# A selective-scan kernel: pairs of state groups scanned in one VectorE instruction over two PSUM banks

## The chip, the cores and the metric

The kernel runs on one core of a Trainium2 chip. The metric is the device time of one execution in microseconds; times are medians of several runs on the same chip. A profile is one execution, recorded by the hardware profiler.

## The reference, cut to what matters

One transformer-like layer on x of 2 x 2048 tokens with 256 features: a modulated layer norm, a bidirectional Mamba mixer, and a mixture of experts. The change touches the mixer's recurrence alone. For each direction it is

```python
def step(h, inp):                       # h: (batch, 512, 16)
    dt_t, u_t, B_t, C_t = inp
    h = h * jnp.exp(dt_t[:, :, None] * A) + (dt_t * u_t)[:, :, None] * B_t[:, None, :]
    y = jnp.einsum('bdn,bn->bd', h, C_t)
    return (h, y)
_, ys = jax.lax.scan(step, h0, xs)      # 2048 tokens, h0 = 0
```

So every one of 512 x 16 states is a first-order recurrence over the tokens: decay times the previous value, plus an input. The result is weighted with C and summed over the 16 states.

## The kernel before, in words

**Steps and units.** The tokens are cut into 8 blocks of 512 (four per batch entry), and forward and backward passes alternate, so there are 16 steps q: even ones forward, odd ones backward. In each step the 512 x 16 states are laid on 128 partitions as 16 units; a unit is four groups (i = 0 to 3) of 128 states, each with 512 tokens along the row. Four units make a chunk of 128 inner channels. All work of the scan stage is counted by the unit T (q = T // 16, t = T % 16). Steps 0, 1, 8 and 9 begin a sequence, so their states start at zero (`q // 2 % SEG == 0`); the other twelve start from states that an earlier step has stored.

**One unit passes through four engines.**
- ScalarE (`decay`, L1225) writes exp(A dt) of group i into PSUM bank PS_A + i, 128x512, four times a unit. It may write a bank when the scan that read it four scans ago is done (`scan_done`).
- VectorE (`multiply`, L1516) writes dbu = (dt u) B, 128x2048, from a PSUM bank and `b_rep` in SBUF. For units t = 3, 7, 9, 11 and 15 (`POOL_UNITS`) GpSimd does it instead (L898), with both inputs in SBUF.
- VectorE (`scan`, L1530) runs the recurrence of one group over 512 tokens: first input the decays in PSUM, second input `dbu` in SBUF, start value 0.0 or a column of `state`, result in the ring `hst` of 7 units.
- ScalarE (`save_state`, L1213) copies the last column of `hst` to `state` (where a later step needs it: all but steps 6, 7, 14 and 15). GpSimd (`weigh`, L910) then multiplies the unit of `hst` in place with `c_rep`; it waits for the scans and for that copy. TensorE (`sum_chunk`, L1949) sums a chunk in PSUM, and VectorE's `gate_y` (L1509) multiplies that with the gate.

**Order.** Every engine's program is written out by hand. VectorE in slot T: the multiplication for unit T+1 (unless it is GpSimd's), then the four scans of T, with a `gate_y` at t = 2, 8, 11 and 15. GpSimd in slot T: the multiplication for T+2 if that is one of its five, then the weighing of T-1, then at four places of a step a 128x512 product (`step_input`, L890). `dbu` has three buffers, so GpSimd's multiplication for T+2 waits for the scans of T-1. ScalarE in slot T: four decays, with the copy of the state of T-1 before the last, and between them its other work (convolution outputs, softplus, SiLU) at (t, n) places given by small tables. TensorE's projections, convolutions and sums run beside.

**Around the stage.** Ahead of it stand the norms (VectorE L1475 to L1496, with GpSimd helping), behind it the experts. The last unit's weighing is VectorE's (L1700).

## Time and profile before

| what | us |
|---|---|
| median of 3 runs | 2182.23 |
| lowest, highest | 2181.46, 2185.82 |
| the profiled execution | 2187.26 |
| its span in the trace | 2185.5 |
| VectorE busy | 2001.1 (92%) |
| GpSimd busy | 1813.4 (83%) |
| TensorE busy | 1896.7 (87%) |
| ScalarE busy | 1390.7 (64%) |

The scan stage reaches from 84 to 1705 us. The page divides the span into 40 slices, of which slices 2 to 31 are this stage. Busy time is the union of an engine's instructions; a duration includes a tail that the next instruction overlaps, so the distance between starts is a little less than the duration.

### The profile page before, as it was taken

What the parts mean: (1) busy time and instruction counts of PE and PEld (TensorE: products, weight loads), DVE (VectorE), ACT (ScalarE), POOL (GpSimd) and SP (SyncE); (2) the same over time, 40 slices, a digit from 0 to 9 for tenths busy, and PEclk for the clock granted to TensorE, in tenths of its full rate; (3) what the DMA queues carried; (4) which work ended last, traced back from release to release, by engine and by line L of the source; (5) the groups of instructions that cost most, each with busy time, mean ns of one, the idle gap of its engine ahead of it and who ended that gap; (6) DMA issues with size and microseconds to landing.
All of it is one profiled execution on the core that took longest, in us unless ns stands there. A gap on an engine that the chain in (4) does not pass through costs nothing.

```text
span 2185.5 us, 25009 instructions
## 1 busy us (share of the span) xinstructions
PE 1896.7 (87%) x6376; PEld 804.2 (37%) x6377; DVE 2001.1 (92%) x2325; ACT 1390.7 (64%) x2540; POOL 1813.4 (83%) x625
## 2 busy tenths in 40 slices
PE   7879898988889898989888898988775799999997
PEld 3323232323233332324232333333221466655554
DVE  7889999999999999999999999999999777557776
ACT  5777868677767768686877777676755333434443
POOL 5599999999999999999999999999999343415444
PEclk9889898989889898989898998989876799999999
DMA  6754535353635444453536253454433552235444
GB/s 257 244 140 123 125 105 126 100 134 86 149 88 131 110 115 120 113 126 105 125 100 150 82 138 99 120 121 113 102 95 133 210 202 81 100 78 84 78 78 69
DMA packets 140339, 265.26 MB, mean 121 GB/s; under 512 B 21264, under 2 KB 44048, under 8 KB 139072
## 3 DMA queue, kind: packets, MB, share of 16 engines
q1 hardware_dynamic: 125488, 242.05, 40.7%
q0 software_dynamic: 13440, 17.93, 4.9%
q10 hardware_dynamic: 1296, 3.93, 0.5%
q8 instruction: 48, 0.79, 0.1%
q14 instruction: 67, 0.55, 0.1%
HBM read 194.51 MB, written 70.39 MB: 121 GB/s over the span
## 4 chain that ended last, share of the span: by engine, by line
DVE 39%; PE 23%; issue 13%; POOL 10%; DMA 6%; ACT 4%; DVEq 2%; SPq 2%; POOLq 0%; ACTq 0%; PEldq 0%
DVE hst L1530 28%; DVE dbu L1516 7%; POOL hst L910 5%; PE psum L2105 5%; POOL dbu L898 4%; PE psum L1949 3%; PE psum L2168 2%; DMA bc_scratch<-sp_tmp 2%; PE psum L2117 2%; PE psum L1869 2%; PE psum L1881 2%; DMA b_rep<-bc_scratch 1%; ACT psum L1225 1%; DVE sz L1509 1%; PE psum L1934 1%
## 5 line engine op out<-in xcount | busy, mean ns | idle before, releaser
L910 POOL TENSOR_TENSOR hst<-hst,c_rep 128x2048 f32<-128x2048 f32 x255 | 1149.8, 4539 | 12.0 <-ACT state L1213 11.4
L1225 ACT ACTIVATE psum<-dt_rep,neg_a 128x512 f32<-128x512 f32 x1024 | 691.4, 684 | 375.5 <-DVE hst L1530 374.2
L1530 DVE TENSOR_TENSOR_SCAN hst<-psum,state,dbu 128x512 f32<-128x512 f32 x768 | 918.3, 1258 | 0.0
L1516 DVE TENSOR_TENSOR dbu<-psum,b_rep 128x2048 f32<-128x2048 f32 x176 | 398.5, 2264 | 8.6 <-PE psum L1934 8.5
L898 POOL TENSOR_TENSOR dbu<-dtu_rep,b_rep 128x2048 f32<-128x2048 f32 x80 | 364.3, 4554 | 29.9 <-DVE hst L1530 29.9
L1934 PE MATMUL psum<-dt,same 32*128 32x512 f32 x352 | 216.4, 696 | 119.2 <-DVE dbu L1516 111.2
L1530 DVE TENSOR_TENSOR_SCAN hst<-psum,dbu 128x512 f32<-128x512 f32 x256 | 291.7, 1199 | 8.1 <-ACT psum L1225 8.1
L1949 PE MATMUL psum<-hst,same 128*32 128x512 f32 x2048 | 258.4, 649 | 16.6 <-POOL hst L910 8.8
L1881 PE MATMUL psum<-xp,taps 128*128 128x512 f32 x512 | 241.2, 615 | 12.4 <-ACT sp_tmp L1196 12.4
L1020 POOL DMA_INDIRECT out_x<-h,target_u x72 | 113.1, 1571 | 154.8 <-DMA out_x<-h,target_u 78.0
L1881 PEld LDWEIGHTS psum<-xp,taps 128*128 128x128 f32 x512 | 96.2, 195 | 153.5 <-issue 153.1
L2168 PE MATMUL psum<-w,h 128*128 x288 | 143.0, 619 | 7.9 <-DVE h L1775 2.2
L984 POOL DMA_INDIRECT slot_scratch<-send,slot_u x64 | 64.3, 1005 | 102.4 <-ACT send L1399 79.4
L1934 PEld LDWEIGHTS psum<-dt,same 32*128 32x128 f32 x352 | 56.1, 197 | 249.6 <-issue 152.2
L1949 PEld LDWEIGHTS psum<-hst,same 128*32 128x32 f32 x2048 | 63.5, 118 | 216.0 <-issue 186.0
L1915 PE MATMUL psum<-sp_tmp,w_dt 16*128 16x512 f32 x128 | 91.9, 832 | 55.8 <-ACT sp_tmp L1181 45.9
L1862 PE MATMUL psum<-xnT,w_in 128*128 128x512 f32 x256 | 126.7, 621 | 8.8 <-ACT xc L1167 7.7
L1869 PE MATMUL psum<-xnT,w_in 128*128 128x512 f32 x256 | 121.3, 606 | 0.6 <-ACT xc L1167 0.6
L1897 PE MATMUL psum<-w_out,sz 128*128 128x256 f32 x512 | 121.1, 391 | 0.0
L2105 PE MATMUL psum<-h2T,sw 128*128 128x512 f32 x256 | 115.0, 603 | 0.9 <-ACT g_silu L1385 0.9
L1897 PEld LDWEIGHTS psum<-w_out,sz 128*128 128x128 f32 x512 | 101.5, 198 | 30.1 <-issue 17.0
L1775 DVE TENSOR_TENSOR h<-psum,b 128x512 f32<-128x512 f32 x72 | 49.8, 691 | 51.0 <-issue 37.1
(183 smaller groups left out, 2418.3 us busy)
## 6 DMA issues: line engine op xcount, KB each, us to landing
dt_rep<-dt_scratch SPq DMA_DIRECT2D x256, 256.0 KB, 4.8
dtu_rep<-dtu_scratch SPq DMA_DIRECT2D x320, 64.0 KB, 1.9
taps<-taps_scratch SPq DMA_DIRECT2D x64, 256.0 KB, 3.2
b_rep<-bc_scratch SPq DMA_DIRECT2D x64, 256.0 KB, 5.0
c_rep<-bc_scratch SPq DMA_DIRECT2D x64, 256.0 KB, 7.8
dt_scratch<-dt SPq DMA_DIRECT2D x63, 256.0 KB, 4.7
h<-slot_scratch SPq DMA_DIRECT2D x72, 129.5 KB
sp_tmp<-t_scratch SPq DMA_DIRECT2D x16, 512.0 KB, 6.8
```

The lines of the kernel that those rows point to most:

```text
L898: nc.gpsimd.tensor_tensor(dbu[:, U % DBU, :, :], dtu_rep[:].broadcast_to((P, NG, TB)), b_rep[U // UNITS % 2][:], ALU.mult).then_inc(pool_m ...
L910: nc.gpsimd.tensor_tensor(h, h, c_rep[q % 2][:], ALU.mult).then_inc(prod_done, 1)
L1225: nc.scalar.activation(psum[:, PS_A + i, :], dt_rep[:, G % 2, j, :], ACT.Exp, scale=neg_a[:, q % 2, u, i:i + 1]).then_inc(exp_done, 1)
L1516: nc.vector.tensor_tensor(dbu[:, U % DBU, :, :], psum[:, PS_U:PS_U + 1, :].broadcast_to((P, NG, TB)), b_rep[U // UNITS % 2][:], ALU.mult). ...
L1530: nc.vector.tensor_tensor_scan(time_order(hst[:, U % RING, i, :], backward), time_order(psum[:, PS_A + i, :], backward), time_order(dbu[:, ...
L1869: ins = nc.tensor.matmul(psum[:, bank, :], w_in[:, q % 2, k, DI + c * P:DI + (c + 1) * P], xnT[:, q % 2, k, :], start=(k == 0), stop=(k == ...
L1881: ins = nc.tensor.matmul(psum[:, bank, :], taps[:, c % 2, j, :], xp[:, c % 2, at:at + TB], start=(j == 0), stop=(j == TAPS - 1))
L1897: ins = nc.tensor.matmul(psum[:, bank, half * DM:(half + 1) * DM], sz[:, c, tok], w_out[:, q % 2, c, :], start=False, stop=(half == 1 and ...
L1934: nc.tensor.matmul(psum[:, PS_U, :], same[part, :], dtu[part, c, :], start=True, stop=True).then_inc(u_full, 1)
L1949: ins = nc.tensor.matmul(psum[CH * j:CH * (j + 1), PS_Y, :], same[:, 0:CH], hst[:, (GN * G + j) % RING, i, :], start=False, stop=(i == NG ...
L2105: ins = nc.tensor.matmul(psum[:, bank, :], w[:, k, c * P:(c + 1) * P], h2T[:, j % 2, k, :], start=(k == 0), stop=(k == KD - 1))
L2168: ins = nc.tensor.matmul(psum[:, 2 + r % 2, :], xtT[:, r % 2, k * P:(k + 1) * P], w13[:, bass.ds(e * KD + k, 1), :].rearrange("p a n -> p ...
```

## The change

One scan instruction takes two groups: 1024 elements a row, over two neighbouring PSUM banks, two rows of `dbu` and two of `hst`. Its start value is always 0.0. So that the second group doesn't continue from the first one's end, the first decay of the second group (in the direction of time) is set to zero in PSUM: `no_decay` writes it once for each pair at t = 0 of a step, and the decays of those banks write 511 columns from then on. Stored states now enter through `dbu`: for each chunk of a step that starts from stored states, ScalarE computes exp(A dt) of the first token (`first_decays`, four 128x4 instructions), VectorE multiplies the 16 stored columns of the chunk by it (`scale_states`, 128x16, in place), and for each unit VectorE adds four columns to the first column of `dbu` (`add_seed`, 128x4). All tensors of these two are in SBUF. ScalarE now computes two decays in a row when a pair of banks is free, the copy of the state moves ahead of them, and two places of softplus move by one.

```diff
-DT_AT = [(10, 0), (10, 3), (12, 0), (13, 1)]
-COPY_DT_AT = [(11, 2), (12, 2), (13, 3), (15, 2)]
+FIRST_DT_AT = [(10, 0), (10, 3), (12, 0), (13, 1)]
+DT_AT = [(9, 3), (10, 3), (12, 1), (13, 1)]
+COPY_DT_AT = [(11, 1), (12, 2), (13, 3), (15, 2)]
...
-                nc.scalar.activation(psum[:, PS_A + i, :], dt_rep[:, G % 2, j, :], ACT.Exp,
+                kept = slice(0, TB) if i % 2 == q % 2 else (slice(1, TB) if q % 2 == 0 else slice(0, TB - 1))
+                nc.scalar.activation(psum[:, PS_A + i, kept], dt_rep[:, G % 2, j, kept], ACT.Exp,
                                      scale=neg_a[:, q % 2, u, i:i + 1]).then_inc(exp_done, 1)
...
+            def no_decay(q, pair):
+                K, at = NG * UNITS * q + 2 * pair, first_of(q)
+                if K >= 4:
+                    act.wait_ge(scan_done, K - 2)
+                nc.scalar.activation(psum[:, PS_A + 2 * pair + 1 - q % 2, at:at + 1], no_halo[:, 0:1], ACT.Copy
+                                     ).then_inc(no_decay_set, 1)
+            def first_decays(G):
...
+                for j in range(GN):
+                    nc.scalar.activation(first_decay[:, j, :], neg_a[:, q % 2, GN * c + j, :], ACT.Exp,
+                                         scale=dt_rep[:, G % 2, j, at:at + 1]).then_inc(first_decay_done, 1)
...
-                    if n == 3 and T > 0 and keeps_state(T - 1):
+                    if n == 2 and T > 0 and keeps_state(T - 1):
                         save_state(T - 1)
-                    decay(T, n)
+                    if n % 2 == 0:
+                        if t == 0:
+                            no_decay(q, n // 2)
+                        decay(T, n)
+                        decay(T, n + 1)
+                    if n == 1 and t % GN == GN - 1 and T + 1 < ALL_UNITS and seeded(T + 1):
+                        first_decays((T + 1) // GN)
...
+            def scale_states(G):
+                q, c = divmod(G, NC)
+                dve.wait_ge(first_decay_done, GN * (seeded_chunks(G) + 1))
+                chunk = state[:, q % 2, GN * c:GN * (c + 1), :, :].rearrange("p u i a -> p (u i a)")
+                nc.vector.tensor_tensor(chunk, chunk, first_decay[:].rearrange("p u i -> p (u i)"), ALU.mult
+                                        ).then_inc(seed_step, 1)
+            def add_seed(U):
+                q, u = divmod(U, UNITS)
+                at = first_of(q)
+                dve.wait_ge(seed_step, seeds(U) - 1)
+                mult_ready(dve, U)
+                first = dbu[:, U % DBU, :, at:at + 1]
+                nc.vector.tensor_tensor(first, first, state[:, q % 2, u, :, :], ALU.add).then_inc(seed_step, 1)
...
-                start = 0.0 if q // 2 % SEG == 0 else state[:, q % 2, u, i, :]
-                dve.wait_ge(exp_done, NG * U + i + 1)
+                dve.wait_ge(exp_done, NG * U + 2 * pair + 2)
+                both = lambda ap: time_order(ap.rearrange("p i t -> p (i t)"), backward)
+                groups = slice(2 * pair, 2 * pair + 2)
                 nc.vector.tensor_tensor_scan(
-                    time_order(hst[:, U % RING, i, :], backward), time_order(psum[:, PS_A + i, :], backward),
-                    time_order(dbu[:, U % DBU, i, :], backward), start, ALU.mult, ALU.add).then_inc(scan_done, 1)
+                    both(hst[:, U % RING, groups, :]), both(psum[:, PS_A + 2 * pair:PS_A + 2 * pair + 2, :]),
+                    both(dbu[:, U % DBU, groups, :]), 0.0, ALU.mult, ALU.add).then_inc(scan_done, 2)
...
-                for i in range(NG):
-                    scan(T, i)
...
+                if on_pool(T) and seeded(T):
+                    add_seed(T)
+                begins = T + 1 < ALL_UNITS and seeded(T + 1)
+                scan(T, 0)
+                if begins and t % GN == GN - 1:
+                    scale_states((T + 1) // GN)
+                if begins and t % GN != GN - 1 and not on_pool(T + 1):
+                    add_seed(T + 1)
...
+                scan(T, 1)
+                if begins and t % GN == GN - 1:
+                    add_seed(T + 1)
```

`seeded(U)` is true in the steps that start from stored states; `seeds(U)` counts these small instructions up to unit U.

VectorE before, in a step that starts from stored states, slots t = 1 to 4 (the multiplications are those for units 2, 4 and 5; unit 3's is GpSimd's; L1509 is the gating):

```order
L1516 TENSOR_TENSOR dbu<-psum,b_rep 128x2048
L1530 SCALAR_TENSOR_TENSOR hst<-psum,state,dbu 128x512 x6
L1509 TENSOR_TENSOR sz<-psum,sz 128x512
L1530 SCALAR_TENSOR_TENSOR hst<-psum,state,dbu 128x512 x2
L1516 TENSOR_TENSOR dbu<-psum,b_rep 128x2048
L1530 SCALAR_TENSOR_TENSOR hst<-psum,state,dbu 128x512 x4
L1516 TENSOR_TENSOR dbu<-psum,b_rep 128x2048
```

VectorE after, the same slots up to the addition for unit 4 (L1593 is `add_seed`, L1583 `scale_states`, L1611 the scan):

```order
L1573 TENSOR_TENSOR dbu<-psum,b_rep 128x2048
L1611 SCALAR_TENSOR_TENSOR hst<-psum,dbu 128x1024
L1593 TENSOR_TENSOR dbu<-dbu,state 128x4
L1611 SCALAR_TENSOR_TENSOR hst<-psum,dbu 128x1024 x2
L1566 TENSOR_TENSOR sz<-psum,sz 128x512
L1611 SCALAR_TENSOR_TENSOR hst<-psum,dbu 128x1024
L1573 TENSOR_TENSOR dbu<-psum,b_rep 128x2048
L1593 TENSOR_TENSOR dbu<-dbu,state 128x4
L1611 SCALAR_TENSOR_TENSOR hst<-psum,dbu 128x1024
L1583 TENSOR_TENSOR state<-state,first_decay 128x16
L1611 SCALAR_TENSOR_TENSOR hst<-psum,dbu 128x1024
L1593 TENSOR_TENSOR dbu<-dbu,state 128x4
```

Twelve scans have become six, and four small instructions of two SBUF inputs stand between them: for 2 between the two scans of 1, for 3 right ahead of its own scan, for 4 behind the scans of 3 with the scaling of its chunk ahead.

ScalarE before, slots t = 10 to 12 (L1225 is a decay, L1194 to L1201 one softplus, L1213 the copy of the state):

```order
L1225 ACTIVATE psum<-dt_rep,neg_a 128x512 x3
L1206 ACTIVATE dt<-psum 128x512
L1213 ACTIVATE state<-hst 128x4
L1225 ACTIVATE psum<-dt_rep,neg_a 128x512
L1134 ACTIVATE xp<-halo 128x3
L1136 ACTIVATE xp<-psum 128x512
L1138 ACTIVATE halo<-xp 128x3
L1225 ACTIVATE psum<-dt_rep,neg_a 128x512
L1194 ACTIVATE dt<-psum,b_dt 128x512
```

ScalarE after, slot t = 12 up to the next pair of decays (L1255 is a decay, L1222 to L1229 the softplus, L1241 the copy):

```order
L1255 ACTIVATE psum<-dt_rep,neg_a 128x511
L1255 ACTIVATE psum<-dt_rep,neg_a 128x512
L1222 ACTIVATE dt<-psum,b_dt 128x512
L1224 ACTIVATE sp_tmp<-psum,b_dt 128x512
L1227 ACTIVATE sp_tmp<-sp_tmp 128x512
L1229 ACTIVATE sp_tmp<-sp_tmp 128x512
L1241 ACTIVATE state<-hst 128x4
L1255 ACTIVATE psum<-dt_rep,neg_a 128x511
L1255 ACTIVATE psum<-dt_rep,neg_a 128x512
```

The decays stand in pairs, and at t = 12 the softplus stands ahead of the copy of unit 11's state. GpSimd's order is the same before and after.

## Rows read from the trace of the kernel before

**Rows 1.** The page: busy us and share by engine; tenths in 40 slices.
```profile
PE 1896.7 (87%) x6376; PEld 804.2 (37%) x6377; DVE 2001.1 (92%) x2325; ACT 1390.7 (64%) x2540; POOL 1813.4 (83%) x625
...
DVE  7889999999999999999999999999999777557776
POOL 5599999999999999999999999999999343415444
```

**Rows 2.** Windows: steps 2 and 9 of the scan stage; columns in the first line.
```profile
core 0: us, PE busy (x) PEld busy (x) DVE busy (x) ACT busy (x) POOL busy (x), PEclk, DMA share, GB/s
...
289.57:391.34 101.77, 86.78 (x290) 32.00 (x290) 101.77 (x80) 73.19 (x129) 101.77 (x26) 0.93 0.47 118
...
999.61:1098.79 99.18, 88.67 (x290) 33.44 (x290) 98.11 (x80) 72.98 (x129) 99.18 (x26) 0.91 0.47 120
```

**Rows 3.** Waits of GpSimd and of VectorE between 84 and 1706 us: total, times, longest.
```profile
POOL dbu L898 <- DVE hst L1530: 29.9, 13, 5.4
POOL hst L910 <- ACT state L1213: 11.4, 11, 4.1
...
DVE hst L1530 <- ACT psum L1225: 8.1, 9, 2.6
```

**Rows 4.** Timeline of VectorE: start, us, instruction; with states, then from zero.
```profile
1257.24 9.49 DVE L1530 TENSOR_TENSOR_SCAN hst<-psum,state,dbu 128x512 f32<-128x512 f32 x8
...
979.06 2.26 DVE L1516 TENSOR_TENSOR dbu<-psum,b_rep 128x2048 f32<-128x2048 f32 x1
981.24 9.01 DVE L1530 TENSOR_TENSOR_SCAN hst<-psum,dbu 128x512 f32<-128x512 f32 x8
...
993.49 0.66 DVE L1509 TENSOR_TENSOR sz<-psum,sz 128x512 f32<-128x512 f32 x1
```

**Rows 5.** Timeline of GpSimd: multiplication, weighings, and the short product.
```profile
1259.68 4.54 POOL L898 TENSOR_TENSOR dbu<-dtu_rep,b_rep 128x2048 f32<-128x2048 f32 x1
1264.18 13.53 POOL L910 TENSOR_TENSOR hst<-hst,c_rep 128x2048 f32<-128x2048 f32 x3
...
905.13 1.28 POOL L890 TENSOR_TENSOR dt<-dt,xc 128x512 f32<-128x512 f32 x1
```

**Rows 6.** Timeline of VectorE behind the stage: short instructions with GpSimd idle.
```profile
1715.37 0.38 DVE L1552 BATCH_NORM_AGGREGATE fmv<-fstats 128x2 f32<-128x6 f32 x4
1715.78 0.17 DVE L1554 TENSOR_SCALAR fvar<-fmv 128x4 f32<-128x4 f32 x1
```

**Rows 7.** Timelines of VectorE and of GpSimd at the stage's end.
```profile
1705.21 6.29 DVE L1700 TENSOR_TENSOR hst<-hst,c_rep 128x2048 f32<-128x2048 f32 x1
...
1695.89 13.46 POOL L910 TENSOR_TENSOR hst<-hst,c_rep 128x2048 f32<-128x2048 f32 x3
```

**Rows 8.** Timelines of VectorE and of GpSimd in the kernel's first 31 us.
```profile
22.66 1.66 DVE L1496 SCALAR_TENSOR_TENSOR H<-H,var,mod 128x256 f32<-128x256 f32 x4
...
28.14 0.90 DVE L1481 TENSOR_SCALAR var<-mv 128x4 f32<-128x4 f32 x1
28.95 1.34 DVE L1490 SCALAR_TENSOR_TENSOR H<-H,mv,mod 128x256 f32<-128x256 f32 x1
...
27.98 1.04 POOL L881 TENSOR_TENSOR diag_d<-ident,d_skip 128x512 f32<-128x512 f32 x1
28.97 1.04 POOL L881 TENSOR_TENSOR diag_d<-ident,d_skip 128x512 f32<-128x512 f32 x1
```

**Rows 9.** Timeline of ScalarE: copy of the state; softplus's first instruction; two decays behind it.
```profile
1254.58 0.21 ACT L1213 ACTIVATE state<-hst 128x4 f32<-128x4 f32 x1 [0.48 <-DVE hst L1530]
...
1259.18 0.67 ACT L1194 ACTIVATE dt<-psum,b_dt 128x512 f32<-128x512 f32 x1
...
1261.65 1.29 ACT L1225 ACTIVATE psum<-dt_rep,neg_a 128x512 f32<-128x512 f32 x2
```

**Rows 10.** Groups by line, 200 to 1640 us: busy, mean ns | idle before.
```profile
L1157 ACT ACTIVATE sz<-sz 128x2048 f32<-128x2048 f32 x14 | 26.7, 1910 | 0.2
...
L1157 ACT ACT_TABLE_LOAD x14 | 18.0, 1283 | 0.2
```

More of the change, by code:

```diff
@@ L134, in keeps_state, with seeded, seeded_chunks, seeds @@
     return U // UNITS // 2 % SEG < SEG - 1
+def seeded(U):
+    return U // UNITS // 2 % SEG > 0
+def seeded_chunks(G):
+    return sum(seeded(GN * g) for g in range(G))
+def seeds(U):
+    G, j = divmod(U, GN)
+    return (GN + 1) * seeded_chunks(G) + j + 2
+def first_of(q):
+    return 0 if q % 2 == 0 else TB - 1
 def states_kept(U):
@@ L241, in mixer_and_experts @@
         c_rep[1] = sb2("c_rep1", [P, NG, TB])
+        first_decay = sb2("first_decay", [P, GN, NG])
         mix.close()
@@ L401, in mixer_and_experts @@
         t_stored = sem("t_stored")
-        zeroed = sem("zeroed")
-        zeros_set = sem("zeros_set")
+        no_decay_set = sem("no_decay_set")
+        first_decay_done = sem("first_decay_done")
+        seed_step = sem("seed_step")
         f_gate_loaded = sem("f_gate_loaded")
@@ L825, in _ @@
                                     base=0, pattern=[[-1, P]], channel_multiplier=1).then_inc(consts, 1)
-            nc.gpsimd.memset(no_halo[:], 0.0).then_inc(zeroed, 1)
+            nc.gpsimd.memset(no_halo[:], 0.0).then_inc(half_set, 1)
             for n, away in enumerate(range(-P + CH, P, CH)):
@@ L1349, in _ @@
                     if ahead:
-                        if (t, n) in DT_AT:
-                            softplus(q + 1, DT_AT.index((t, n)))
+                        if (t, n) in (DT_AT if q > 0 else FIRST_DT_AT):
+                            softplus(q + 1, (DT_AT if q > 0 else FIRST_DT_AT).index((t, n)))
                         if (t, n) in COPY_DT_AT:
@@ L1518, in multiply, with scan @@
                                         b_rep[U // UNITS % 2][:], ALU.mult).then_inc(vector_mult_done, 1)
-            def scan(U, i):
+            def scale_states(G):
+                q, c = divmod(G, NC)
+                dve.wait_ge(first_decay_done, GN * (seeded_chunks(G) + 1))
[4 more added lines that the diff above has]
+                q, u = divmod(U, UNITS)
+                at = first_of(q)
+                dve.wait_ge(seed_step, seeds(U) - 1)
+                mult_ready(dve, U)
+                first = dbu[:, U % DBU, :, at:at + 1]
+                nc.vector.tensor_tensor(first, first, state[:, q % 2, u, :, :], ALU.add).then_inc(seed_step, 1)
+            def scan(U, pair):
                 q, u = divmod(U, UNITS)
                 backward = q % 2 == 1
-                if i == 0:
+                if pair == 0:
                     mult_ready(dve, U)
+                    if seeded(U):
+                        dve.wait_ge(seed_step, seeds(U))
                     if U >= RING:
                         dve.wait_ge(chunk_summed, (U - RING) // GN + 1)
-                start = 0.0 if q // 2 % SEG == 0 else state[:, q % 2, u, i, :]
-                dve.wait_ge(exp_done, NG * U + i + 1)
+                if u == 0:
+                    dve.wait_ge(no_decay_set, 2 * q + pair + 1)
+                dve.wait_ge(exp_done, NG * U + 2 * pair + 2)
+                both = lambda ap: time_order(ap.rearrange("p i t -> p (i t)"), backward)
+                groups = slice(2 * pair, 2 * pair + 2)
                 nc.vector.tensor_tensor_scan(
-                    time_order(hst[:, U % RING, i, :], backward), time_order(psum[:, PS_A + i, :], backward),
-                    time_order(dbu[:, U % DBU, i, :], backward), start, ALU.mult, ALU.add).then_inc(scan_done, 1)
+                    both(hst[:, U % RING, groups, :]), both(psum[:, PS_A + 2 * pair:PS_A + 2 * pair + 2, :]),
+                    both(dbu[:, U % DBU, groups, :]), 0.0, ALU.mult, ALU.add).then_inc(scan_done, 2)
             def row(n, j, count):
@@ L1685, in _ @@
                             dve.wait_ge(p1_norm, NT * (n + 1))
-                for i in range(NG):
-                    scan(T, i)
-                    if i == 1:
-                        if t == 2 and q > 0:
-                            gate_y(q - 1, 3)
-                        if t == 11:
-                            gate_y(q, 1)
-                    if i == 0 and t == 15:
-                        gate_y(q, 2)
+                if on_pool(T) and seeded(T):
[6 more added lines that the diff above has]
+                    add_seed(T + 1)
+                if t == 2 and q > 0:
+                    gate_y(q - 1, 3)
+                if t == 11:
+                    gate_y(q, 1)
+                if t == 15:
+                    gate_y(q, 2)
+                scan(T, 1)
+                if begins and t % GN == GN - 1:
+                    add_seed(T + 1)
                 if t == 8:
```

5 lines of the change are left out of this document (4 added, 1 removed).

## The prediction

> **What bounds the kernel now.** Read the page's busy shares and slices first [rows 1]. Over most of the span VectorE and GpSimd both stand at 9 tenths or more; TensorE and ScalarE don't. Then the windows, cut at every 16th unit of the scan stage (a "step") [rows 2]: a step that starts from stored states (2 to 7 and 10 to 15) lasts 101.77 us, all of it VectorE's; in the steps that start from zero GpSimd is as near: step 9 lasts 99.18 us, all of it GpSimd's. The waits [rows 3] say the same: between 84 and 1706 us VectorE waits 8.1 us for decays and hardly for anything else, GpSimd 29.9 us for VectorE's scans and 11.4 for the copies behind them.
>
> VectorE's 101.77 us add up. Eight scans with states in a row take 9.49 us, so one comes each 1.176 us (the last one's tail of 0.08 us off); without states eight take 9.01, one each 1.116 [rows 4]. The multiplication starts 2.18 us before its successor (979.06 to 981.24), the gating product 0.58 (0.66 without its tail). A step has 64 scans, 11 multiplications, 4 gatings: 75.3 + 24.0 + 2.3 = 101.6. GpSimd's product comes each 4.50 us, its 512-column product 1.23 (1.28 without the tail) [rows 5]: 16 weighings, 5 multiplications, 4 short ones are 94.5 + 4.9 = 99.4 us. So at best, with VectorE much faster, a stateful step gives back 2.4 us before GpSimd is the bound.
>
> **What the change takes away.** The gating product has 512 columns and takes 0.58, the multiplication 2048 and takes 2.18: 1.04 ns a column and 0.05 us fixed. If the scan's fixed part is the same 0.05, its 512 columns cost 1.066 us and 1024 cost 2.18. No scan of 1024 columns over two banks is in the trace; the bounds are 2.13 (nothing fixed) and 2.23 (twice 1.116), and I take 2.18 because two other lengths give that fixed part. A stateful step then has 32 x 2.18 + 24.0 + 2.3 = 96.1 us on VectorE, 5.6 less; a step from zero 96.1 too, 1.8 less than its 97.9.
>
> **What it adds on VectorE.** In each stateful step, 16 additions of 128x4 (`add_seed`) and 4 products of 128x16 (`scale_states`). Four short statistics instructions in a row take 0.38 us, one each 0.08 with the tail off; a short one that waits for the instruction before it takes 0.17 and the next starts a few hundredths later [rows 6]. So 0.08 where nothing near waits (14 of the 20), 0.20 where the scan behind waits at once (6): 2.3 us. By these alone a step has 98.4 us on VectorE and GpSimd's 99.4 would bound it.
>
> **What they wait for.** These 20 are of a kind that the scan stage has not had: both their inputs lie in SBUF. A scan and a multiplication take one from PSUM. The end of the stage shows one such instruction beside GpSimd [rows 7]: the last weighing, on VectorE, starts at 1705.21, waits for nothing by the record, and lasts 6.29 us, against 2.26 for a multiplication of its size. GpSimd's last product ends at 1695.89 + 13.46 = 1709.35, and 1709.35 + 2.14 = 1711.49 is where VectorE's ends. It stood until GpSimd's instruction was over. The start of the kernel shows it for shorter ones [rows 8]: four 128x256 operations with two SBUF inputs take 1.66 us undisturbed; the one at 28.95 takes 1.34 alone, and ends 0.28 after GpSimd's product from 28.97 to 30.01. A 128x4 TENSOR_SCALAR at 28.14 takes 0.90 instead of 0.17 and ends at 29.04, where GpSimd's previous product ends, though another starts right behind. So VectorE gets in between two GpSimd instructions and waits for the rest of one, not for a pause.
>
> The Trainium skill (SBUF — State Buffer, "Who interferes with whom") has the rule: a VectorE instruction with two SBUF inputs contends with a GpSimd instruction that reads SBUF, the lock is exclusive, and the loser blocks for the whole instruction whatever its shape. The trace agrees for the large ones; that the rule holds for a `tensor_tensor` of four elements no row shows. By the rule the sum is the one below, without it the first rival's.
>
> So each of the 20 waits for the rest of GpSimd's current instruction: from 0 to 4.5 us. Which, I lay out for one step, VectorE's order (after) beside GpSimd's, which is unchanged. A weighing may start when the last scan of its unit has ended and ScalarE has copied the state: 0.2 us of copy and a hop on either side [rows 9], 0.4 in all. A GpSimd multiplication for unit T+2 (3, 7, 9, 11 and 15) stands ahead of the weighing of T-1 and starts 0.1 after T-1's last scan. "After" below is the time from that last scan.
> - Ordinary (the additions for 1, 5, 13): multiplication and scan, 4.36 us; the weighing runs from 0.4 to 4.9. Wait 0.4. For 2, 6 and 14 a GpSimd multiplication runs from 0.1 to 4.6: wait 0.2.
> - From unit 1 GpSimd has a queue: multiplication to 4.6, weighings to 9.1, 13.6, 18.1. VectorE has two multiplications, four paired scans, a gating and a wait of 0.2 before the addition for 3 and comes at 13.9, 0.3 us into the weighing that began at 13.6: wait 4.3. After 5 and after 12 there is no gating on that way: the additions for 7 and 15 come at 13.3, inside the weighing before: 0.4 each. One scan later the scaling for the next four units comes at 15.9, inside the GpSimd instruction that began at 14.8 (the short product lies between): 3.4 each, for 8 and for 0.
> - Behind 7, still counted from 5, the scaling lets go at 19.3 and a scan ends at 21.5, inside the weighing from 19.3 to 23.8: the addition for 8 waits 2.4. The scans of 8 end at 28.2; GpSimd's multiplication for 11 runs from 28.4 to 32.9, and the addition for 9 comes at 31.0 (after gating and multiplication): 1.9. A scan on, 35.1, the weighing runs to 37.3: 2.2 for 10. Then 39.5, 43.8 after the scans of 10, 46.0 after the multiplication, and a weighing from 44.4 to 48.9: 2.9 for 11. In the other five places (scalings for 4 and 12, additions for 4, 12 and 0) GpSimd is idle: 0.08 each.
> - The addition for 13 waits 1.0 longer: ScalarE's softplus, 2.5 us (1259.18 to 1261.65), now stands between the decays and the state's copy, so that weighing begins later.
>
> Together 3 x 0.4 + 1.0 + 3 x 0.2 + 4.3 + 2 x 0.4 + 2 x 3.4 + 2.4 + 1.9 + 2.2 + 2.9 + 0.4 = 24.5. A step lasts 96.1 + 24.5 = 120.6 us. In steps 6, 7, 14 and 15 no state is kept, GpSimd starts 0.3 sooner where it was idle and there is no such copy: 22.4, so 118.5. VectorE is then the only bound, since GpSimd's 99.4 fits.
>
> **ScalarE** gets two instructions more a step (the zero decays) and 16 short ones (0.2 each), and can refill two banks only when a pair is done. One pair of decays takes 1.3 us, a scan 2.18, and most slots have a multiplication too. The tightest place is the SiLU of z (1.9 us and two table loads of 1.3 [rows 10], 4.5) behind unit 7: 1.5 + 4.5 + 1.3 = 7.3 after the scan of 6, where the scan of 8 may start at 6.9; with the waits above it starts later anyway. I cost it at nothing; in a step from zero it can cost 0.4.
>
> **The sum**, against the profiled run of 2187.26: 8 steps x (120.6 - 101.8) = +150.4; 4 x (118.5 - 101.8) = +66.8; steps 0, 1, 8, 9 -1.6, -1.6, -2.9 and -2.0 (the last nears GpSimd's pace) = -8.1; the last weighing waits 0.3 instead of 4.1: -3.8. That is +205.3, 2392.6. The profiled run lies 5.0 above the median, 2182.23; against the median, **2388**.
>
> **Rivals.**
> - *The short ones don't wait.* Then VectorE has 98.4 us a step, GpSimd 99.4, and GpSimd bounds: 12 x 2.4 = 29 less, and some 3 in the steps from zero: 2150. For it: no row has a four-element `tensor_tensor` beside GpSimd. Against: the 0.90 us of rows 8. It decides at a mean wait of 0.17 us over the 20: VectorE's 3.4 us of gain are then used up. 8%.
> - *They meet GpSimd anywhere.* My layout has margins of 0.3 us (the addition for 3). With mean waits of half an instruction, 20 x 2.27 us times GpSimd's busy share 99.4/T: T = 98.4 + 4513/T, T = 132.5. 12 x 30.7 - 12 = +356: 2538. For it: each wait shifts all behind it. Against: a weighing starts from the scan it needs, which pulls the two into step each unit. 6%.
> - *The addition for 3 comes 0.3 earlier*, and slips into the gap: 4.2 less a step, 50 in all: 2338. Also the scalings for 8 and 0: down to 2260. 5% below 2330.
> - *The paired scan saves nothing* (2.23): VectorE 1.6 more a step, in part inside the waits: 2395, in the range.
>
> **How the numbers follow.** The layout, with its bounds, 81%. Its range goes from the slipped addition, 2338, to 5 us more a step, 2450; I set 2330 to 2460. About 0.2%, 4.4 us, is what a measurement of this kernel can tell from none; nothing of mine ends within it except by accident. Slower 0.91, same 0.01, faster 0.08.
>
> **What would show it.** After: the 128x4 additions on VectorE have a mean far over 0.2 us, up to 4.5, each ending where a GpSimd instruction ends; the stateful windows are 118 to 122 us, the zero-start ones 96 to 99; GpSimd waits some 20 us a step for VectorE; the scan comes each 2.18. Additions of 0.16 us beside a running GpSimd product would prove it wrong, as would scans that wait for ScalarE's decays.

## The result

The kernel after takes **2474.88 us** (median of 4 runs, 2472.83 to 2477.29) against 2182.09 of the kernel before in the same job: ratio 1.1331, 95% interval [1.1315, 1.1348]. The forecast was 2388 with a range up to 2460. The sign was right, and so was the mechanism that makes most of the loss; the time is 87 us longer than forecast. The profiled run of after has a span of 2471.1 us.

The page of after (columns as in [rows 1]): VectorE's share is the same 91%, GpSimd's fell from 83 to 73%. In the steps that start from stored states GpSimd stands at 7 or 8 tenths instead of 9; it waits. It keeps its 9 only around the steps from zero (slices 3 to 5 and 18 to 20).

```profile
PE 1967.4 (80%) x6376; PEld 834.4 (34%) x6377; DVE 2239.1 (91%) x2053; ACT 1419.3 (57%) x2764; POOL 1815.7 (73%) x625
...
DVE  8899999999999999999999999999999986747776
POOL 5699977777777878899978788787878843424444
```

Windows of after, steps 2 and 9, as in [rows 2]. A stateful step went from 101.77 to 125.37 us (120.6 was forecast), step 9 from 99.18 to 107.03 (under 99 was forecast).

```profile
293.67:419.04 125.37, 96.68 (x290) 36.28 (x290) 121.45 (x69) 76.04 (x148) 99.45 (x26) 0.83 0.35 89
1142.22:1249.25 107.03, 89.46 (x290) 33.85 (x290) 102.14 (x51) 73.37 (x137) 101.64 (x27) 0.90 0.47 121
```

Groups of after on VectorE, 84 to 2010 us (busy, mean ns | idle before). The paired scan shows 2.28 us with its tail; where two stand in a row they begin 2.20 us apart (2.18 was forecast). The 192 additions of four columns have a mean of 1.21 us, the 48 scalings 1.88: together 321.7 us. Those that met an idle GpSimd took 0.13 to 0.15 each.

```profile
L1611 DVE TENSOR_TENSOR_SCAN hst<-psum,dbu 128x1024 f32<-128x1024 f32 x512 | 1151.7, 2275 | 25.9 <-ACT psum L1255 11.8 <-issue 10.1 <-POOL dbu L926 4.1
...
L1593 DVE TENSOR_TENSOR dbu<-dbu,state 128x4 f32<-128x4 f32 x192 | 231.6, 1206 | 0.0
L1583 DVE TENSOR_TENSOR state<-state,first_decay 128x16 f32<-128x16 f32 x48 | 90.1, 1877 | 0.0
```

Timelines of VectorE and GpSimd, beginning of step 2. The additions for 1, 2 and 3 take 0.54, 0.42 and 4.20 (0.4, 0.2 and 4.3 were forecast). The one at 312.59 ends at 316.79; GpSimd's three weighings of 4.50 each run from 303.26 to 316.76. It ended where GpSimd ended. So do nearly all: 168 of the 240 small instructions come while a GpSimd instruction runs, and 165 of them end within 0.1 us of its end.

```profile
302.90 0.42 DVE L1593 TENSOR_TENSOR dbu<-dbu,state 128x4 f32<-128x4 f32 x1
...
312.59 4.20 DVE L1593 TENSOR_TENSOR dbu<-dbu,state 128x4 f32<-128x4 f32 x1
...
303.26 13.50 POOL L938 TENSOR_TENSOR hst<-hst,c_rep 128x2048 f32<-128x2048 f32 x3
```

The waits of after, as in [rows 3], 84 to 2010 us. GpSimd waits 323.5 us for VectorE's scans and the copies behind them (41.3 before). In a stateful step it is idle for 26 us (125.37 less 99.45 in step 2), where some 20 were forecast. New is the first row. VectorE waits 33.9 us for TensorE at the multiplication for unit 6 (6.6 at its multiplications before), once in each of steps 1 to 14.

```profile
DVE dbu L1573 <- PE psum L2023: 33.9, 15, 3.4
DVE hst L1611 <- ACT psum L1255: 11.8, 11, 2.6
...
POOL hst L938 <- ACT state L1241: 183.9, 64, 5.6
POOL hst L938 <- DVE hst L1611: 72.6, 20, 5.8
POOL dbu L926 <- DVE hst L1611: 67.0, 44, 4.9
```

Where that wait comes from stands in the timelines of ScalarE and TensorE, slot 4 of step 3. L1195 copies the last convolution chunk out of the PSUM bank that the second output projection (L1982, L1986) needs. It stands behind the first decays of unit 4; these are now two, and wait until a whole pair of banks is free, so the copy starts at 446.00. TensorE waits 4.97 us for it and comes late to the spreading of unit 6 (L2023).

```profile
444.76 1.30 ACT L1255 ACTIVATE psum<-dt_rep,neg_a 128x511 f32<-128x511 f32 x2 [7.46 <-DVE hst L1611]
446.00 0.67 ACT L1195 ACTIVATE xc<-psum,b_conv 128x512 f32<-128x512 f32 x1
...
446.72 2.08 PE L1982 MATMUL psum<-sp_tmp,ident 128*128 128x512 f32 x2 [4.97 <-ACT xc L1195]
...
454.53 1.12 PE L2023 MATMUL psum<-dt,same 32*128 32x512 f32 x2
```

VectorE pays twice for it. It waits 1.54 us itself (1.4 to 3.4 across steps 1 to 14), and the additions for 6 and 7, which come later by that much, fall into the next GpSimd instruction: 3.30 and 4.17 us here, where 0.2 and 0.4 were forecast.

```profile
455.69 2.29 DVE L1573 TENSOR_TENSOR dbu<-psum,b_rep 128x2048 f32<-128x2048 f32 x1 [1.54 <-PE psum L2023]
...
460.09 3.30 DVE L1593 TENSOR_TENSOR dbu<-dbu,state 128x4 f32<-128x4 f32 x1
...
472.06 4.17 DVE L1593 TENSOR_TENSOR dbu<-dbu,state 128x4 f32<-128x4 f32 x1
...
454.32 4.55 POOL L926 TENSOR_TENSOR dbu<-dtu_rep,b_rep 128x2048 f32<-128x2048 f32 x1 [2.40 <-DVE hst L1611]
458.83 4.53 POOL L938 TENSOR_TENSOR hst<-hst,c_rep 128x2048 f32<-128x2048 f32 x1
```

### The profile page after: what moved, and what is told of

Read it like the earlier page. It is cut to its first block and busy times, and to the rows that moved or that the text cites. A ratio compares the mean times of both kernels' runs of the same rounds, so it can differ in the third digit from the quotient of the medians.

```text
span 2471.1 us, 25718 instructions
## 1 busy us (share of the span) xinstructions
PE 1967.4 (80%) x6376; PEld 834.4 (34%) x6377; DVE 2239.1 (91%) x2053; ACT 1419.3 (57%) x2764; POOL 1815.7 (73%) x625
## 5 line engine op out<-in xcount | busy, mean ns | idle before, releaser
L1611 DVE TENSOR_TENSOR_SCAN hst<-psum,dbu 128x1024 f32<-128x1024 f32 x512 | 1151.7, 2275 | 25.9 <-ACT psum L1255 11.8
L1255 ACT ACTIVATE psum<-dt_rep,neg_a 128x512 f32<-128x512 f32 (+1 forms) x1024 | 661.9, 678 | 481.4 <-DVE hst L1611 480.6
L2023 PE MATMUL psum<-dt,same 32*128 32x512 f32 x352 | 230.1, 738 | 194.6 <-DVE dbu L1573 186.4
L1970 PE MATMUL psum<-xp,taps 128*128 128x512 f32 x512 | 259.4, 654 | 14.5 <-ACT sp_tmp L1224 14.5
L1593 DVE TENSOR_TENSOR dbu<-dbu,state 128x4 f32<-128x4 f32 x192 | 231.6, 1206 | 0.0
L2023 PEld LDWEIGHTS psum<-dt,same 32*128 32x128 f32 x352 | 58.6, 205 | 321.8 <-issue 193.0
L1970 PEld LDWEIGHTS psum<-xp,taps 128*128 128x128 f32 x512 | 103.7, 210 | 173.0 <-issue 172.4
L1012 POOL DMA_INDIRECT slot_scratch<-send,slot_u x64 | 64.4, 1006 | 102.4 <-ACT send L1456 79.3
L1986 PE MATMUL psum<-w_out,sz 128*128 128x256 f32 x512 | 137.1, 429 | 0.0
L1241 ACT ACTIVATE state<-hst 128x4 f32<-128x4 f32 x192 | 39.1, 204 | 155.7 <-DVE hst L1611 154.6
L1986 PEld LDWEIGHTS psum<-w_out,sz 128*128 128x128 f32 x512 | 114.6, 224 | 40.8 <-issue 23.2
```

The lines of the kernel that those rows point to most:

```text
L1255: nc.scalar.activation(psum[:, PS_A + i, kept], dt_rep[:, G % 2, j, kept], ACT.Exp, scale=neg_a[:, q % 2, u, i:i + 1]).then_inc(exp_done, 1)
L1593: nc.vector.tensor_tensor(first, first, state[:, q % 2, u, :, :], ALU.add).then_inc(seed_step, 1)
L1611: nc.vector.tensor_tensor_scan(both(hst[:, U % RING, groups, :]), both(psum[:, PS_A + 2 * pair:PS_A + 2 * pair + 2, :]), both(dbu[:, U % D ...
L1970: ins = nc.tensor.matmul(psum[:, bank, :], taps[:, c % 2, j, :], xp[:, c % 2, at:at + TB], start=(j == 0), stop=(j == TAPS - 1))
L1986: ins = nc.tensor.matmul(psum[:, bank, half * DM:(half + 1) * DM], sz[:, c, tok], w_out[:, q % 2, c, :], start=False, stop=(half == 1 and ...
L2023: nc.tensor.matmul(psum[:, PS_U, :], same[part, :], dtu[part, c, :], start=True, stop=True).then_inc(u_full, 1)
```

## The experiments

Medians; ratios are against the kernel before in the same job: 2185.7 us beside e1 to e4, 2183.0 beside e5 to e8 and `e6_seeds_on_scalar`, 2185.0 beside e9 to e11 and `e6b_seeds_on_scalar`.

| run | edit against after | us | ratio, 95% interval |
|---|---|---|---|
| e1_no_seeds | no small instructions | 2174.8 | 0.9947 [0.9925, 0.9969] |
| e2_one_input | small ones with one input | 2195.8 | 1.0036 [1.0009, 1.0064] |
| e3_four_scans | four scans again, small ones stay | 2457.9 | 1.1257 [1.1200, 1.1315] |
| e4_seeds_behind | small ones behind a unit's last scan | 2435.5 | 1.1154 [1.1090, 1.1219] |
| e5_spread_first | TensorE spreads unit 6 first | 2470.3 | 1.1310 [1.1275, 1.1345] |
| e9_conv_earlier | ScalarE's copy one pair earlier | 2414.5 | 1.1057 [1.1039, 1.1076] |
| e7_probe | 30 more small ones, steps 1 and 9 | 2499.9 | one run |
| e8_no_seeds_spread | e1 and e5 | 2222.6 | 1.0175 [1.0152, 1.0199] |
| e10_no_seeds_conv | e1 and e9 | 2155.2 | 0.9864 [0.9848, 0.9881] |
| e6_seeds_on_scalar | states by start value and ScalarE, and e5 | 2246.3 | 1.0277 [1.0251, 1.0304] |
| e6b_seeds_on_scalar | the same without e5 | 2212.3 | 1.0122 [1.0102, 1.0141] |
| e11_scalar_conv | the same with e9 | 2164.9 | 0.9911 [0.9894, 0.9927] |

### Is it the small instructions, and is it their second input?

`e1_no_seeds` drops them; the stored states then never enter.

```diff
-                if on_pool(T) and seeded(T):
-                    add_seed(T)
...
-                if begins and t % GN == GN - 1:
-                    scale_states((T + 1) // GN)
```

> The paired scans alone: the additions, the scalings and ScalarE's first decays are left out, so stored states don't enter. If the loss is the wait of the two-input instructions for GpSimd's, a stateful step falls from 125.4 us to about 100 (VectorE 96.1 and the two waits, for TensorE 2.4 and for the decays 1.5, that the steps from zero show) and the kernel comes to 2155 to 2170 us. If the paired scan or the paired decays are at fault, it stays above 2300.

`e2_one_input` keeps all 240 in place and in number, as reductions that read one SBUF tensor; here too the states don't enter.

```diff
-                nc.vector.tensor_tensor(first, first, state[:, q % 2, u, :, :], ALU.add).then_inc(seed_step, 1)
+                nc.vector.tensor_reduce(state[:, q % 2, u, 0, :], state[:, q % 2, u, :, 0], axis=AX_X, op=ALU.add
+                                        ).then_inc(seed_step, 1)
```

> All 20 small instructions of a step stand where they stood, with the same semaphores, but each is a reduction with one SBUF input (128x4 or 128x16 to one column of the state) in place of a product or sum of two; stored states don't enter. If the second SBUF input makes them wait for GpSimd, each lasts about 0.17 us wherever it falls, a stateful step is 102 to 103 us and the kernel 2185 to 2200 us. If any small instruction between two scans costs as much (a drained pipeline, a chain of semaphores), their mean stays near 1.2 us and the kernel near 2475.

The group of `e2_one_input` on VectorE that answers to L1593:

```profile
L1592 DVE TENSOR_REDUCE state<-state 128x1 f32<-128x4 f32 x192 | 26.0, 135 | 0.0
```

0.135 us each beside the same GpSimd work, against 1.206. A stateful step lasts 102.4 us, against 125.4. So 23.0 of the 23.6 us that a step lost go with the second SBUF input, and the first rival (the short ones don't wait) is out. The run also changed the operation and where it writes; that these matter by themselves is not excluded by it alone, but the 165 of 168 ends above leave them little room. `e1_no_seeds` is a little above its range, and its waits (84 to 1640 us) say why: TensorE is late there as well.

```profile
DVE dbu L1573 <- PE psum L2013: 44.6, 17, 3.8
DVE hst L1609 <- ACT psum L1255: 27.3, 21, 2.6
```

### Is it the pairing of the scans?

`e3_four_scans` scans each group alone, start value zero, single decays, and keeps the small instructions:

```diff
-                    if n % 2 == 0:
-                        if t == 0:
-                            no_decay(q, n // 2)
-                        decay(T, n)
-                        decay(T, n + 1)
+                    decay(T, n)
...
+                scan(T, 2)
+                scan(T, 3)
```

> The small instructions without the pairing: four scans of 512 from 0.0 with decays one by one as before, the seeds added at the same places. If the seeds' waits are the loss and the wait for TensorE at the multiplication for unit 6 (2.3 us a step) comes from the paired decays, that wait is gone, a stateful step is about 120.3 us and the kernel 2400 to 2420. If the wait for TensorE comes from the seeds' delays, it stays: 124 to 125 us a step, 2465 to 2480. If the seeds cost little, it lies near 2200.

It came between the two expectations, and its steps fall into two kinds. In steps 5 and 13 VectorE does not wait for TensorE; they last 120.8 us, with 0.42 and 0.16 for the additions for 6 and 7 and 3.37 for the scaling for 8: the pattern of the forecast. In steps 2 to 4 and 10 to 12 it waits 0.65 to 1.19 us there, and they last 125.7, with 3.6 to 4.1 for the addition for 6 and 4.05 for that for 7. Under 1.2 us of wait costs 5. That pointed to TensorE's delay as what carries the additions across a boundary of GpSimd (the moment between two of its instructions).

The run also shows that pairing is not the only thing that makes the copy L1195 late. These are TensorE's waits for that copy at the second output projection, in the scan stage of before, of `e1_no_seeds` (pairs, no small instructions), of `e3_four_scans` (small instructions, no pairs) and of after (both):

```profile
PE psum L1893 <- ACT xc L1167: 16.1, 14, 1.5
...
PE psum L1972 <- ACT xc L1195: 40.8, 14, 2.9
...
PE psum L1976 <- ACT xc L1195: 44.3, 13, 4.9
...
PE psum L1982 <- ACT xc L1195: 71.0, 14, 6.6
```

1.2 us each time before, 2.9 with the pairs alone, 3.4 with the small instructions alone, 5.1 with both. The small instructions delay the scans, and the decays ahead of the copy wait for those.

### Another place for the small instructions

```diff
-                if on_pool(T) and seeded(T):
-                    add_seed(T)
...
+                    scale_states((T + 1) // GN)
+                if begins:
```

> The same instructions, all moved to one place: directly behind the last scan of the unit before, where GpSimd often has just run dry and starts 0.1 to 0.4 us later. If a wait is set by where in GpSimd's instruction an addition arrives, the same layout gives 113.8 us a stateful step instead of 124.9, and the kernel about 2340 us. If the wait is a property of the instruction or of its number, nothing changes: 2475.

Missed by 95 us. Steps 2 to 5 and 10 to 13 last 118 to 119, steps 6 and 14 130.8 and step 7 126.3. Additions that were short became long (medians: for 2 2.69 us, for 8 4.41, for 14 2.50) while the one for 3 fell to 0.14: many waits were moved, not removed. In steps 6 and 14 the additions for 4, 12 and 0 take 4.5 each, against 0.17 in the steps that keep their states: without the copy of the state GpSimd has started 0.02 us before they come.

### TensorE's delay, taken away in two ways

`e5_spread_first` moves one matmul ahead of the late projections:

```diff
                     if t == 4:
+                        spread_input(T + 2)
                         project_out(q - 1, 1)
```

> One matmul moved on TensorE: at t = 4 the spreading of dt u for unit 6 (one matmul of 32x512) goes ahead of the output projection and the z projection it stood behind. If the wait of 2.3 us at unit 6's multiplication is what carries the additions for 6 and 7 over a boundary of GpSimd's instructions, then with that wait gone they wait 0.2 and 0.4 us (now 2.3 and 3.8), the scaling for 8 waits 3.4 and the addition for 8 2.4, a stateful step is 120 to 121 us instead of 125.4, and the kernel 2400 to 2420 us. If the positions of these waits come from something else, only the 2.3 us go: 2440 to 2450.

Neither came about. The wait for TensorE is gone, and the additions for 6 and 7 fell to 0.42 and 0.24, as forecast. But VectorE's waits for decays grew. In `e5_spread_first`, 84 to 1990 us (11.8 in after):

```profile
DVE hst L1611 <- ACT psum L1255: 87.6, 46, 3.6
```

`e8_no_seeds_spread` makes the same move in the kernel without small instructions, to see it without GpSimd's boundaries:

> The paired scans alone, stored states left out, with the matmul for unit 6 ahead: what the pairing could bring with free seeds. VectorE's 44.6 us of waits for TensorE go for the most part, GpSimd's 99.4 us a step bounds, 2150 to 2165 us. If TensorE's wait only moves to another place, it stays at 2175.

It missed as well, and the same way: 48 us slower than `e1_no_seeds`, with 116.6 us of waits for decays. Step 3 of it shows why, on VectorE, TensorE and ScalarE:

```profile
418.92 2.26 DVE L1573 TENSOR_TENSOR dbu<-psum,b_rep 128x2048 f32<-128x2048 f32 x1
...
439.55 2.29 DVE L1609 TENSOR_TENSOR_SCAN hst<-psum,dbu 128x1024 f32<-128x1024 f32 x1 [3.59 <-ACT psum L1255]
...
421.23 2.07 PE L2013 MATMUL psum<-dt,same 32*128 32x512 f32 x2 [4.47 <-DVE dbu L1573]
423.23 2.08 PE L1972 MATMUL psum<-sp_tmp,ident 128*128 128x512 f32 x2
...
418.15 0.67 ACT L1195 ACTIVATE xc<-psum,b_conv 128x512 f32<-128x512 f32 x1
...
437.56 0.60 ACT L1175 ACTIVATE sz<-psum 128x512 f32<-128x512 f32 x1 [4.47 <-PE psum L1948]
```

The moved matmul has a wait of its own. It writes the bank that VectorE's multiplication for unit 5 still reads (`vector_mult_done`), and that ends at 421.18. TensorE's program runs in order, so the output projection now stands behind this wait. Its bank had been free since 418.82, but it begins at 423.23, 26.8 us into the step, against 22.4 in `e1_no_seeds`. The z projections, ScalarE's copies of z and the decays behind those copies follow late. The move put a later wait in the place of the bank's.

`e9_conv_earlier` frees the bank earlier instead, by one entry of ScalarE's table:

```diff
-CONV1_AT, XP2_AT, XP3_AT, CONV2_AT, CONV3_AT = (0, 1), (0, 3), (1, 0), (2, 0), (4, 0)
+CONV1_AT, XP2_AT, XP3_AT, CONV2_AT, CONV3_AT = (0, 1), (0, 3), (1, 0), (2, 0), (3, 3)
```

> The kernel after with one table entry changed: ScalarE copies the last convolution chunk of the next step behind the decays of unit 3 instead of behind the first pair of unit 4, so that TensorE's second output projection finds its bank free and the spreading of unit 6 is not late. Theory A (VectorE's 2.3 us wait for TensorE per step is what moved the additions for 6 and 7 across a boundary of GpSimd, and its source is that copy): steps go from 125.4 to about 121, the addition for 6 back to 0.2-0.5, that for 7 to 0.2-0.5, time 2400-2425 us. Theory B (as when the spreading itself was pulled ahead: the next late stage, ScalarE's decays, takes the wait over): VectorE waits for TensorE under 10 us in all but over 40 us for decays, time 2450-2480 us. Theory C (the bank is not what TensorE waits for): same waits as after, 2470-2478 us.

2414.5 us: theory A. The waits of VectorE, 84 to 1950 us, the window of step 2, and timelines of ScalarE, TensorE and VectorE in step 3, all of `e9_conv_earlier`:

```profile
DVE hst L1611 <- ACT psum L1255: 11.2, 12, 2.6
...
DVE dbu L1573 <- PE psum L2023: 3.2, 1, 3.2
...
293.64:414.04 120.40, 92.62 (x290) 34.11 (x290) 119.28 (x69) 75.94 (x148) 99.37 (x26) 0.85 0.38 96
...
432.28 0.67 ACT L1195 ACTIVATE xc<-psum,b_conv 128x512 f32<-128x512 f32 x1
...
435.89 1.12 PE L1982 MATMUL psum<-sp_tmp,ident 128*128 128x512 f32 x2
...
453.40 0.45 DVE L1593 TENSOR_TENSOR dbu<-dbu,state 128x4 f32<-128x4 f32 x1
...
462.52 0.32 DVE L1593 TENSOR_TENSOR dbu<-dbu,state 128x4 f32<-128x4 f32 x1
```

TensorE finds its bank free, nothing takes the wait over, and a stateful step lasts 120.4 us, where the forecast's layout gave 120.6. The durations (us) by the unit for which an instruction stands, median of steps 2 to 5 and 10 to 13 (e9 is `e9_conv_earlier`; the four that are not shown, for 4, 12 and 0 and the scaling for 4, take 0.13 to 0.15 in both kernels):

| | 1 | 2 | 3 | 5 | 6 | 7 | scaling 8 | 8 | 9 | 10 | 11 | scaling 12 | 13 | 14 | 15 | scaling 0 |
|---|---|---|---|---|---|---|---|---|---|---|---|---|---|---|---|---|
| forecast | .4 | .2 | 4.3 | .4 | .2 | .4 | 3.4 | 2.4 | 1.9 | 2.2 | 2.9 | .08 | 1.4 | .2 | .4 | 3.4 |
| e9 | .55 | .42 | 4.21 | .57 | .45 | .30 | 3.30 | 2.33 | 2.02 | 2.09 | .15 | 2.17 | .55 | .42 | .35 | 3.30 |
| after | .55 | .43 | 4.20 | .65 | 2.73 | 4.16 | 2.08 | .13 | 2.02 | 2.08 | .15 | 2.17 | .56 | .42 | .36 | 3.31 |

The two kernels differ in four places, for 6 to 8, by 2.7 us together. That e9's step is so near the forecast is in part luck. The layout had the addition for 11 at 2.9 and the scaling for 12 at 0.08; they took 0.15 and 2.17. The reason stands on GpSimd's timeline of `e9_conv_earlier`: the weighing of unit 10 waits for ScalarE's copy of the state. That copy stands behind a softplus, two decays, the four first decays and a copy of dt, and comes 1.9 us after unit 10's last scan. The weighing begins only when the addition for 11 is over.

```profile
495.51 0.15 DVE L1593 TENSOR_TENSOR dbu<-dbu,state 128x4 f32<-128x4 f32 x1
...
495.68 4.52 POOL L938 TENSOR_TENSOR hst<-hst,c_rep 128x2048 f32<-128x2048 f32 x1 [1.70 <-ACT state L1241]
```

### What the first scaling waits for

In steps 1 and 9 the scaling for the next step is the first of the small instructions (the addition for unit 0 follows it), and it takes longer than any GpSimd instruction. VectorE and GpSimd in `e9_conv_earlier`:

```profile
280.63 8.03 DVE L1583 TENSOR_TENSOR state<-state,first_decay 128x16 f32<-128x16 f32 x1
...
273.92 9.03 POOL L938 TENSOR_TENSOR hst<-hst,c_rep 128x2048 f32<-128x2048 f32 x2
282.90 1.28 POOL L918 TENSOR_TENSOR dt<-dt,xc 128x512 f32<-128x512 f32 x1
284.12 4.51 POOL L938 TENSOR_TENSOR hst<-hst,c_rep 128x2048 f32<-128x2048 f32 x1
```

It passed two boundaries of GpSimd (282.9 and 284.1) and got in at the third, 288.6. `e7_probe` puts a small two-input maximum of a tensor with itself into each of the first 15 units of those two steps:

```diff
                 scan(T, 0)
+                if q in (1, 9) and t < UNITS - 1:
+                    dve.wait_ge(state_saved, 1)
...
+                    nc.vector.tensor_tensor(spot, spot, spot, ALU.max).then_inc(probed, 1)
```

> The changed kernel with one more VectorE instruction in each of the first 15 units of steps 1 and 9, behind the unit's first scan: a 128x4 maximum of the stored state of unit 0 with itself, two SBUF inputs, nothing that waits for its result but the scaling at the step's end. In these steps GpSimd runs without a pause and units behind VectorE. If a waiting VectorE instruction always gets in at the end of GpSimd's current one, each lasts at most 4.5 us and the first of them is like the rest. If it only gets in when GpSimd has nothing left that is ready (as the 5.5 us of the first scaling in steps 1 and 9 suggest), the first lasts as long as GpSimd's whole backlog, 8 to 20 us, and the later ones, with the backlog gone, are short; and the scaling at the end of these steps then lasts 4.5 us or less.

The thirty last 0.16 to 4.28 us, none longer than one GpSimd instruction, and the scaling behind them 3.7 in both steps. So the small instructions of these steps do not wait for GpSimd's whole run in general. One exception is among the probes: the first of step 9 comes at 1152.27, passes the boundary at 1154.97 and ends at 1156.24, with the next GpSimd instruction; the first of step 1 got in at the next boundary. The probes and the shifts behind them cost 8.5 us in step 1 and 21.5 in step 9. Why the first scaling passes boundaries in the other kernels (5.5 us in after, 8.0 in `e9_conv_earlier`, up to 10.0 in `e4_seeds_behind`) stays open. Of the small instructions of after that came while GpSimd ran with another instruction right behind, 86 of 89 got in at the next boundary; the other three are these two and the addition for 9 in step 15 (7.20 us).

### What pairing is worth, and a version that beats both

> The same moved copy in the kernel whose stored states never enter (no scaling, no addition; scans in pairs), which took 2174.8 us with 44.6 us of VectorE's waits for TensorE and 27.3 us for decays in its scan stage. This leaves out the carry of the state between steps. Theory A (the copy is the source): TensorE's 44.6 us go to about 10, time 2135-2150 us, so that pairing alone is worth 2 per cent once nothing is late. Theory B (the wait is handed to the decays, as with the spreading ahead): 2170-2225 us.

2155.2, 5 us above theory A's range. The window of step 4 shows the floor that the expectation forgot; the next row is `e11_scalar_conv`'s, same step:

```profile
485.30:584.40 99.10, 87.70 (x290) 32.10 (x290) 96.57 (x48) 72.59 (x132) 99.10 (x26) 0.91 0.46 118
...
485.50:586.00 100.50, 85.99 (x290) 31.74 (x290) 98.40 (x48) 84.38 (x180) 99.32 (x26) 0.92 0.46 117
```

VectorE has 96.57 us of work (96.1 was forecast without the small ones), and GpSimd 99.10 of 99.10: it bounds, as the prediction said it would. Pairing gives 1.4% here, with the stored states left out.

`e6_seeds_on_scalar`, `e6b_seeds_on_scalar` and `e11_scalar_conv` bring the stored states in without VectorE: the scan's start value for the first group, and one ScalarE instruction of one column for each second group.

```diff
+                    nc.scalar.activation(spot, state[:, q % 2, u, i, :], ACT.Identity, bias=spot,
+                                         scale=first_decay[:, U % GN, i:i + 1]).then_inc(seed_step, 1)
...
+                    start = state[:, q % 2, u, 2 * pair + q % 2, :]
```

> The paired scan without any two-input instruction on VectorE: the first group of a pair starts from its stored column as before the change (the scan's start value, 0.06 us more), the second group's first input column is made by ScalarE (two 128x1 instructions a unit: state times first decay plus the input); the matmul for unit 6 ahead as in the run above. VectorE 98.0 us a stateful step, GpSimd's 99.4 bounds: 99.5 to 101 us a step against 101.8 before, the kernel 2150 to 2170 us, 0.6 to 1.5% faster than before. If ScalarE's 32 further instructions delay decays, VectorE's waits for them grow and it lies at 2180 or above.

> The stored states enter without VectorE's small instructions: the first group by the scan's start value, the second group's first column made by ScalarE; TensorE's order as in the kernel after. The run with TensorE's order changed as well took 2246.3 us and its counterpart without stored states 2222.6, a difference of 24 us (448 scans with a start value from memory at 0.06 us each are 27 us). Theory A (the difference carries over to TensorE's old order): 2174.8 + 24 = 2195-2205 us, slower than before by under 1 per cent. Theory B (ScalarE, with two more small instructions per unit, falls behind and VectorE waits for it): 2225-2260 us. Faster than before, 2150-2178 us, would need the start value to be free beside the waits.

> Stored states by start value and ScalarE, and the copy of the last convolution chunk behind the decays of unit 3. Theory A (the copy is the source of TensorE's wait, and nothing takes the wait over): about 30 us under the run without the moved copy, 2160-2180 us, which would beat the kernel before. Theory B (ScalarE's decays are late instead): 2200-2250 us.

The first missed by 76 us: with TensorE's order changed it has `e8_no_seeds_spread`'s waits for decays. The second, at 2212.3, lies 7 us above theory A's range and below B's; TensorE's delay is still in it. The third is within theory A: **2164.9 us, 0.9% faster than before**, and it computes the whole reference. Two groups and one wait of it:

```profile
L1626 DVE TENSOR_TENSOR_SCAN hst<-psum,state,dbu 128x1024 f32<-128x1024 f32 x384 | 878.3, 2329 | 25.4 <-ACT dbu L1276 25.0 <-ACT psum L1255 0.3
...
L1626 DVE TENSOR_TENSOR_SCAN hst<-psum,dbu 128x1024 f32<-128x1024 f32 x127 | 283.1, 2269 | 12.2 <-ACT psum L1255 12.2
...
DVE hst L1626 <- ACT dbu L1276: 25.0, 12, 2.2
```

A start value from SBUF costs 0.06 us a scan, 23 us in 384. With it VectorE has 98.40 us of work in step 4, and 25 us of waits for ScalarE's column, once in each stateful step, bring the step to 100.5.

## Why the prediction was right in direction and wrong in size

- *The paired scan, 2.18 us:* right within 0.02 us (2.20). So were the 0.20 for a small instruction that the scan behind waits for (a gap of 0.19 at six places a step) and the floor of GpSimd's 99 us.
- *The 20 small instructions wait for the rest of GpSimd's current instruction:* right, 23 us a step by `e2_one_input`. The rule of the Trainium skill (SBUF — State Buffer, "Who interferes with whom") holds for four elements as it does for 2048: 4.20 us for a 128x4 addition, and the reduction with one input takes 0.135.
- *Which they are:* in `e9_conv_earlier` each duration is within 0.3 us of the layout but for three. The addition for 11 is 2.75 less and the scaling for 12 2.1 more, which nearly cancel, by luck: ScalarE's other work delays the copy of unit 10's state, where I had such a delay at 13 alone. The addition for 13 is 0.9 less.
- **"ScalarE [...] I cost it at nothing":** the step that failed. I had checked the decays against the scans, and only behind the SiLU of z. What else stands in ScalarE's row behind a decay was not followed to who waits for it: the copy at (4, 0) frees TensorE's bank. TensorE's wait for it went from 1.2 us a step to 5.1, by the pairs of decays and by the small instructions' own delay of the scans. It costs 5.0 us a step in after (125.5 against 120.5 with the copy moved): some 2.1 of VectorE's wait (the mean of these eight steps) and 2.7 of longer small instructions. I also named only VectorE and GpSimd in the layout and gave it margins for no other engine, though TensorE was 87% busy [rows 1] and VectorE already waited 6.6 us for it before, which the prediction passed over as "hardly for anything else".
- *Steps without a kept state, 118.5:* wrong. Steps 6 and 14 last 120.3 and 120.6 in `e9_conv_earlier`: the earlier start changes several waits (13: 0.26 instead of 0.55, 11: 2.64 instead of 0.15, scaling 12: 0.15 instead of 2.17), and they nearly cancel. Steps 7 and 15 are short (116.8 and 118.6), 7 since it holds no addition and scaling for the next step. Step 15 I had also set against 101.8, and it lasted 97.5 before.
- *The working of steps from zero:* 64 scans of 1.116 with 24.0 and 2.3 are 97.7, not 97.9; it changes nothing that counts.
- *Steps 0, 1, 8 and 9, -8.1 us:* they came to +13.7 in after and +9.7 in `e9_conv_earlier`. Steps 1 and 9 already hold the scaling for the step behind them, which I left out: 5.5 us each in after, 8.0 in `e9_conv_earlier`. And VectorE's wait for decays in steps 1 and 9 is 1.5, not 0.4; TensorE's wait, 2.4 to 3.4 us, falls on steps 1, 8 and 9 of after too.

By size, in profiled spans (after is 80.3 us over the forecast's sum): the eight stateful steps of the first kind 39.2, steps 6, 14, 7 and 15 20.4, steps from zero 21.8, what stands before and behind the stage -1.1. With the copy moved the total is 21 over: -0.7, 6.6, 17.8 and -2.7 in the same order. So the failed step cost some 59 us of the 80, and the time without it, 2414.5, lies in the range that was given. The largest part of the other 21 is the scaling in steps 1 and 9.

## What to carry to other kernels

Here a VectorE instruction whose inputs both lie in SBUF cost the rest of GpSimd's current instruction, at 4, 16 and 2048 columns alike; beside a busy GpSimd give it one input, one in PSUM, or another engine. When an engine's instructions are fused or paired, follow every instruction behind them in its row to the engine that waits for it, the banks it frees above all. Before you move an instruction ahead of one that waits, look what it waits for itself: in an in-order program all behind it inherits that wait. In a layout of two engines in step, a delay of 1 us by a third can cost 5: give the range the price of one slipped boundary at each place.

## What the runs showed that I had not expected

- Between two back-to-back GpSimd instructions VectorE's waiting instruction gets in at the first boundary in 86 of 89 cases of after; exceptions reach 10 us (`e4_seeds_behind`), cause open.
- Moving one matmul ahead made a kernel 48 us slower (`e8_no_seeds_spread` against `e1_no_seeds`), since it brought its own wait for VectorE along; moving one copy of 0.67 us made it 20 us faster (`e10_no_seeds_conv`).
- A start value read from SBUF costs a 1024-element scan 0.06 us, 2.33 against 2.27, as much as it costs one of 512 [rows 4].
